# A joint key-and-score product on five stacked arrays of 128 rows in place of six, with the left sides of the mixer on VectorE and the exponentials one step later

## What is computed

```
x = x + xattn(ctx_768, layernorm(x), mask, ...)   # 4 heads of 64; 1601 context tokens of 192 channels per batch
x = x + attn(layernorm(x), ...)                   # token mixer: a recurrence with 4 heads
x = x + ffn(layernorm(x), ...)                    # 16 experts, 4 picked, and a shared one

# xattn, what matters here
xn = layernorm(ctx) * g + b;  ln = layernorm(latents) * g + b
q = ln @ Wq.T;  k, v = [xn @ Wkv.T ; ln @ Wlkv.T] split in halves
attn = rmsnorm(q) * SCALE @ rmsnorm(k).T, masked, softmax over 1601 + 64 keys
out = (attn @ v) @ Wo.T + bo
```

## Time and profile before

| | |
|---|---|
| time, median of 3 runs | 528.2 us (527.94 to 531.03) |
| the profiled execution | 528.14 us, of which the span is 526.4 us |
| mean granted TensorE clock | 0.958 |
| attention loop (first to last `kr`) | 50.8 to 328.1 us |
| token mixer, then experts | about 348 to 439 us, then to the end |
| busy: PE, PEld, DVE, ACT, POOL | 456.7, 358.0, 372.4, 217.5, 269.9 us |
| key-and-score matmuls | 624, of the 828 in the largest PE group |

### The profile page before, as it was taken

The page is one execution under the profiler, slowest core; times in us unless marked ns, Lnnn a source line. Parts: engine busy times, 40 slices in busy tenths (PEclk is TensorE's granted clock), DMA queues, the critical chain, the costliest instruction groups (busy, mean ns, idle before and its releaser), DMA issues.

```text
span 526.4 us, 6598 instructions
## 1 busy us (share of the span) xinstructions
PE 456.7 (87%) x2146; PEld 358.0 (68%) x2146; DVE 372.4 (71%) x850; ACT 217.5 (41%) x471; POOL 269.9 (51%) x261
## 2 busy tenths in 40 slices
PE   3787787998989989989989989788899787789996
PEld 0464555876877877868778768685366665678885
DVE  5746576787887888878876775533568756887776
ACT  0236443554554545654445534231053025335551
POOL 5454868659568576595685543001372232435550
PEclk9999988799999999999999979896999899989999
DMA  7705970051231501514000000920000000000001
GB/s 237 184 1 135 249 183 2 1 140 49 59 82 49 138 9 44 140 50 96 0 2 0 2 0 7 396 108 0 1 0 1 0 0 1 0 2 2 0 2 40
DMA packets 23590, 31.74 MB, mean 60 GB/s; under 512 B 2674, under 2 KB 19268, under 8 KB 23556
## 3 DMA queue, kind: packets, MB, share of 16 engines
q1 hardware_dynamic: 23556, 31.32, 21.3%
HBM read 30.69 MB, written 0.52 MB: 59 GB/s over the span
## 4 chain that ended last, share of the span: by engine, by line
DVE 30%; PE 29%; POOL 25%; issue 11%; ACT 3%; DMA 1%; SPq 0%; DVEq 0%; POOLq 0%; ACTq 0%
PE bank L565 28%; POOL kr L469 16%; DVE kss L1368 5%; DVE arena L1380 5%; DVE arena L1416 5%; POOL crs L440 3%; POOL split_b L463 2%; DVE kguard L1371 2%; DVE arena L1576 1%; DVE arena L1562 1%; DMA mask_in<-in_p_mask 1%; POOL cve L439 1%; POOL cguard L441 1%; DVE arena L1418 1%; DVE cst L1313 1%
## 5 line engine op out<-in xcount | busy, mean ns | idle before, releaser
L565 PE MATMUL bank<-keyq,split_b 96*128 96x512 f32 (+2 forms) x828 | 198.2, 390 | 14.6 <-DVE split_b L1633 9.7
L565 PEld LDWEIGHTS bank<-keyq,split_b 96*128 96x128 f32 (+2 forms) x828 | 147.3, 196 | 47.8 <-DVE split_b L1633 11.6
L469 POOL TENSOR_TENSOR kr<-kguard,neg_half 128x8 f32<-128x8 f32 (+1 forms) x56 | 87.1, 1555 | 95.4 <-DVE kguard L1371 94.9
L565 PE MATMUL bank<-arena 128*128 128x193 f32 (+4 forms) x528 | 104.7, 343 | 11.7 <-ACT arena L1116 6.9
L565 PEld LDWEIGHTS bank<-arena 128*128 128x128 f32 (+2 forms) x528 | 89.0, 198 | 24.2 <-ACT arena L1116 11.3
L1380 DVE TENSOR_TENSOR arena<-bank,kr 128x512 f32<-128x512 f32 (+1 forms) x56 | 36.6, 653 | 58.0 <-POOL kr L469 58.0
L463 POOL TENSOR_TENSOR split_b<-arena,split_b 98x512 fp32r<-98x512 f32 (+1 forms) x56 | 65.4, 1169 | 7.5 <-ACT split_b L1092 7.5
L1116 ACT ACTIVATE arena<-arena 128x512 f32<-128x512 f32 x48 | 30.2, 631 | 75.5 <-DVE arena L1416 75.5
L1109 ACT ACTIVATE arena<-bank 128x512 f32<-128x512 f32 (+1 forms) x56 | 31.5, 563 | 51.3 <-PE bank L565 51.0
L565 PE MATMUL bank<-split_b,keyq 128*128 128x512 f32 x204 | 49.6, 393 | 0.1
L565 PEld LDWEIGHTS bank<-split_b,keyq 128*128 128x128 f32 x204 | 37.5, 190 | 7.4 <-DVE split_b L1624 0.2
(11 more groups left out here) (216 smaller groups left out, 598.7 us busy)
## 6 DMA issues: line engine op xcount, KB each, us to landing
arena<-in_p_ctxT SPq DMA_DIRECT2D x8, 1200.8 KB, 8.8
arena<-in_ctx SPq DMA_DIRECT2D x16, 576.0 KB, 4.9
arena<-in_p_experts SPq DMA_DIRECT2D x1, 2688.0 KB, 18.2
arena<-in_p_experts SPq DMA_DIRECT2D x1, 2304.0 KB, 12.5
arena<-in_p_experts SPq DMA_DIRECT2D x1, 1536.0 KB, 7.1
X<-in_x SPq DMA_DIRECT2D x1, 512.0 KB, 4.1
arena<-in_t_Wlkv SPq DMA_DIRECT2D x1, 512.0 KB, 8.9
out<-arena SPq DMA_DIRECT2D x4, 128.0 KB, 1.8
```

Source lines behind the costliest of these rows:

```text
L469: pool.tensor_tensor(kr[0:r, n % 2, 0:k], kg_[0:r, n % 2, 0:k], neg_half[0:r, 0:4 * k].rearrange("p (t h) -> p t h", h=H), ALU.pow).then_i ...
L565: return nc.tensor.matmul(out_, l, r, start=start, stop=stop, skip_group_check=shared)
```

## The change

**Channels.** The 192 context channels are divided 128 and 64 (`CH`) in place of 96 and 96. The second array holds 64 channels, two rows of the standard deviation (high part and low part, both by DMA), the mask row, zeros up to row 96, and in rows 96 to 127 half of the low part of its own 64 channels. Two such copies exist, one with the lower and one with the upper 32 channels' low part. The weights have matching rows (`twin`, on ACT, copies 32 rows of the high part of keyq to rows 96 to 127). A tile's product then is five matmuls, (high0, high0), (high0, low0), (twin A, twin A), (twin B, low with twin B), (low0, high0), ten per group in place of twelve, each with 128 rows.

**Splitting.** `split_high` is two ACT instructions (128 x 256, and 96 x 512 which writes both copies). `split_rest` is three POOL instructions: 128 x 256, a wait for its own completion, then twice 32 x 256 from partitions 0 to 31 or 32 to 63 into 96 to 127, and a wait again. `sd_low` is new on POOL (13 x 128, at g = 4), `evac_sd` has two ACT instructions, and `spread_sd` has two DMAs and waits for `sd_low`. The turned context and Wkv each come by two DMAs.

**Order.** `SUM` is NG + 4, so exponentials and context_sum come one step later; `evac_sum` moves from g = 2 to g = 3 and `evac_latent_out` from 3 to 4 on DVE; shift_scores follows key_sums at g = 2 and 3. In the mixer the left sides move to DVE, each ahead of the right side of its level; on POOL `gate_up_low(0)`, `gate_up_low(1)` and `down_low(0)` move behind the scales of the group norm, between and behind the two `rstd`.

The core of the diff:

```diff
-        SUM = NG + 3
+        SUM = NG + 4
...
-                pool.tensor_tensor(xs_low[n % 3][:, :, 0:k], ctxT[b % 2][:, :, 256 * g:256 * g + k], xs_high[n % 3][:, :, 0:k].bitcast(F32), ALU.subtract).then_inc(xs_rest, 1)
+                v, raw = xs[n % 3], ctxT[b % 2][:, :, 256 * g:256 * g + k]
+                then(pool.tensor_tensor(v[:, 1, 0:k], raw[:, 0], v[:, 0, 0:k].bitcast(F32), ALU.subtract))
+                for j in range(2):
+                    last = pool.tensor_tensor(v[96:P, 2 + j, 0:k], raw[32 * j:32 * j + 32, 1], v[32 * j:32 * j + 32, 2 + j, 0:k].bitcast(F32), ALU.subtract)
+                last.then_inc(xs_rest, 1)
+                pool.wait_ge(xs_rest, n + 1)
...
+                if g == 4 and b + 1 < B:
+                    sd_low(b + 1)
...
-                    for s, (x_, w_) in enumerate(((xs_high, 0), (xs_low, 0), (xs_high, 1))):
-                        for c in range(2):
-                            d = DEPTH[c]
-                            last = mm(bank[0:rows(t), key_banks(n) + i, :], x_[n % 3][0:d, c, i * P:i * P + rows(t)],
-                                      keyq[0:d, c, w_, 0:slot + 1:slot, :], s == 0 and c == 0, s == 2 and c == 1)
+                    for s, (x_, w_) in enumerate(((0, 0), (0, 1), (2, 2), (3, 3), (1, 0))):
+                        last = mm(bank[0:rows(t), key_banks(n) + i, :], xs[n % 3][:, x_, i * P:i * P + rows(t)],
+                                  keyq[:, w_, 0:slot + 1:slot, :], s == 0, s == 4)
...
-                A(xs_high[n % 3][:, :, 0:k], ctxT[b % 2][:, :, 256 * g:256 * g + k], ACT.Copy).then_inc(xs_split, 1)
+                A(xs[n % 3][:, 0, 0:k], ctxT[b % 2][:, 0, 256 * g:256 * g + k], ACT.Copy)
+                A(xs[n % 3][0:96, 2:4, 0:k], ctxT[b % 2][0:96, 1:2, 256 * g:256 * g + k].broadcast_to([96, 2, k]), ACT.Copy).then_inc(xs_split, 1)
...
-                sp.wait_ge(sdT_evac, b + 1)
+                sp.wait_ge(sd_rest, b + 1)
...
-                if g != 2 and 0 <= u - SHIFT < groups:
+                if g not in (2, 3) and 0 <= u - SHIFT < groups:
                     shift_scores(u - SHIFT)
...
                 if lv + 2 < LEVELS:
+                    left_side(lv + 2)
                     right_side(lv + 2)
```

158 lines of the change are left out of this document (92 added, 66 removed).

## The result

The changed kernel takes **557.0 us** (median of 4 runs, 556.4 to 558.2), the kernel before 529.15 (median of 4): a ratio of 1.054 (95% interval 1.050 to 1.057), 28 us slower. The forecast was 551, with a range of 532 to 575. The profiled execution spans 555.2 us where it was 526.4. Every ratio in this text leaves out executions more than 1.5% above the fastest of their kernel (one of ten of e_moved_by_act_circle, three of ten of e_moved_late), and every median has all of them.

What follows compares the result with a forecast made beforehand. The prediction took the circle of DVE and POOL, not PE, as the bound. Loop 19.4, deviations 4, start 1.3, drain -1.3 and mixer -0.2 summed to +23.2 us on 528.14, so 551, with a range of 532 to 575.

Steps and rivals of the forecast that it cites:

- The split's parts: POOL's split in the attention loop: 0.73 us for each part, narrow ones too, so three take 2.2 against 1.27.
- Full steps with a shift: Attention-loop steps g = 5, 6 and the next 0: each costs 0.24 us more, with DVE's maximum going first.
- g=1 to 2: Loop step where POOL is the longer arm: 0.8 us more in each of seven batches.
- The first batch: First batch of the attention loop, without shifts: 2.2 us more.
- g=2 to 4: Loop steps with the new DVE order, the short split and sd_low: together +0.3 us a batch.
- The rule against the row: Shift of g = 3 during kr: the trace row lets it run at once (551); the port rule holds it (557).
- The deviations' way: DMA of the standard deviations waits for sd_low, making DVE's squares at g = 5 late: 0.6 us in seven batches, 4.
- Start: Chain to the first keys: ACT's extra split instructions and twin copies cost +1.3 us, at most 2.5.
- Drain: End of the loop: PE's wait for an exponential goes with exponentials a step later, -1.3 us.
- win the ties: Rival: POOL's second split part goes ahead of DVE's maximum in about 20 steps, +13 us, so 564; chance 0.18.
- The clock: Rival: PE's granted clock falls in the loop, one episode in each of six batches, +15 us, so 566; chance 0.10.
- Narrow parts: Rival: POOL's 32-row split parts are cheap, 0.3 us each, time near 536 or 531; chance 0.18.

Runs made afterwards that it cites:

- e_moved_by_act_circle: Changed kernel with POOL's low parts in two instructions, ACT copying the 32-row pieces, and DVE's shift and maximum behind the next step's sums: 528.5 us.
- e_moved_late: e_moved_by_act_circle with ACT's copies at the head of its next step and POOL's g=2 scales ahead of its split: 532.9 us.
- e_before_five: Kernel before with the last of the six matmuls of each tile left out: 527.2 us, ratio 0.999.
- e_before_split3: Kernel before with only POOL's split cut into three instructions of 256 elements a row, with waits: 558.6 us, ratio 1.057.
- the split in one: Changed kernel with POOL's three split instructions put together to one of 128 x 512, output differing: 523.3 us, ratio 0.990.
- e_after_no_sdlow: Changed kernel without the low part of the standard deviations, the high part sent twice as soon as ACT has it: 552.2 us, ratio 1.045.
- e_before_circle: Kernel before with DVE's shift and running maximum both behind the next step's key sums: 511.1 us, ratio 0.970.

## Why the prediction was right, point by point

**The bound.** Right: DVE and POOL's circle, not PE. e_before_five shows it by itself, and the waits in both kernels agree.

**Matmuls at nothing.** Right: -0.6 us with an interval of -2.2 to +1.0, in place of 27.

**The split's parts.** Right in size and in the reason for it. By form, from 54 to 356 us (columns: count, busy us, mean ns, idle before). The means hold the waits behind DVE; one alone stands in the timeline with 0.74:

```profile
L472 POOL TENSOR_TENSOR split_b<-arena,split_b 32x256 fp32r<-32x256 f32 x90 | 83.8, 931 | 6.2
...
L470 POOL TENSOR_TENSOR split_b<-arena,split_b 128x256 fp32r<-128x256 f32 x45 | 35.9, 797 | 7.1 <-ACT split_b L1109 7.1
```

```profile
184.38 0.74 POOL L472 TENSOR_TENSOR split_b<-arena,split_b 32x256 fp32r<-32x256 f32 x1
```

A part of 32 partitions takes 0.74 and one of 128 takes 0.73, so the height and the move between partitions cost nothing. e_before_split3 shows that this edit alone makes a loss as large as the change's.

**The loop.** Forecast +23.4 (19.4 and 4 for the deviations), measured +29.9. This is the term that was too small, in three places. (a) Full steps with a shift: 0.24 held for g=4 to 5 (5.17 against 4.92 without the deviations), but g=5 to 6 and 6 to 0 took 0.35 (0.46 in every second batch at 6 to 0). The sum counted on full key sums (0.67) covering POOL's third part; at g=5 to 6 the sums have 65 rows and take 0.40 (timeline above), the third part ends later than they do, and kr waits for it. (b) g=1 to 2: +1.26 in place of 0.8. The sum had the third part end 2.63 behind kr and cve right behind it. The second part is held by the maximum and takes 1.26, and cve starts 2.93 behind kr, 1.73 later than before in place of 1.39. The sum also gave cve 0.4 back, as if it were no longer held. It still is, by the shift, which is itself held by the third part, so cve gives back only 0.12; but cguard, held before, takes 0.26 in place of 0.59, which the sum did not have. So what comes back, 0.45, is right in size by luck, and the parts are what cost more. In the changed kernel:

```profile
175.72 2.06 POOL L472 TENSOR_TENSOR split_b<-arena,split_b 32x256 fp32r<-32x256 f32 x2
177.86 0.57 POOL L445 TENSOR_SCALAR cve<-cmv 128x7 f32<-128x7 f32 x1
...
180.10 0.26 POOL L447 TENSOR_SCALAR cguard<-cve 128x7 f32<-128x7 f32 x1
...
177.10 1.22 DVE L1435 TENSOR_TENSOR arena<-arena,side 128x512 f32<-128x512 f32 x1
```

and before, behind the cve of the earlier trace rows:

```profile
199.12 0.59 POOL L441 TENSOR_SCALAR cguard<-cve 128x7 f32<-128x7 f32 x1
```

(c) The first batch: 37.2 against 31.8, +5.4, where I had 2.2 and 0.6 for the deviations. Without shifts DVE's arm is short, and POOL's three parts are the longer one; 1.3 of the 5.4 goes with the deviations (the batch takes 35.9 without them). Places (a) and (b) make the 4.8 us by which batches two to seven exceed 6 x 3.3, (c) the other 2.6; the last batch, -0.1 in place of +1.0, gives 1.1 back. That last number is luck. In the kernel before, g=3 to 4 of the last batch took 7.15 us with the slow stretch of the earlier trace rows in it, and 4.79 after. Without these 2.4 us, for which the sum had no term, the loop's forecast would have been further off.

**g=2 to 4.** Forecast +0.3, measured +0.09. The price of the parts is +0.49 (e_before_split3), and the new order on DVE, with the shift in the time of kr, gives 0.41 back.

**The rule against the row.** The forecast went by the row (kr doesn't hold the shift) and not by the rule's 557. The row was right about that: g=2 to 3 fell from 5.19 to 4.59 with the move. That the time came out at 557 is no proof of the rule; it is (a) to (c). But the rule's other half, a DVE instruction that holds kr, I had not thought of.

**The deviations' way.** Forecast +4, measured 4.8 by taking it away. The size was right, the path wrong: I had DVE waiting for squares, but it is POOL's first part that waits for ACT's split (shown above). It also isn't a price of its own, as the split in one hides all but 0.27 us in each of the first two batches.

**Start, drain, mixer.** Start: forecast +1.3, measured -0.6 (the first kr stood at 50.0 to 51.1 in the six kernels that start as the one before does, so this is hardly more than their scatter); no cost of the twins' copies shows. Drain: forecast -1.3, measured -0.6 from the last kr to the last sum (23.4 to 22.8). Rest: forecast -0.2, measured +0.2.

**The rivals.** POOL did not win the ties: 32 of the 40 maxima of 128 x 512 ran free in 0.69 us, the others took 0.85; in the step shown the lead was 0.01 us. (The prediction named an unheld maximum as a sign of being wrong. That contradicts its own sum, which has the maximum go first, and by the sum it was right.) The clock did fall, once in every batch from the third on, and cost nothing there. Two stretches of the changed kernel (last columns: granted clock, DMA share, GB/s):

```profile
140.00:150.00 10.00, 8.89 (x32) 7.46 (x33) 7.01 (x16) 2.58 (x8) 8.57 (x12) 0.66 0.24 65
150.00:160.00 10.00, 8.39 (x49) 7.16 (x48) 8.19 (x19) 6.73 (x18) 8.13 (x7) 1.00 0.01 2
```

The steady batches are 39.5 to 39.9 us with it, and DVE waits for squares 3.0 us in the whole loop: slack in PE pays for it. But the cover was thin. In these batches the clock was low for 6.8 us at a time; in e_before_split3 and e_after_no_sdlow, stretches of 10.2 us that reached into g=3 to 4 cost 0.65 to 1.3 each, six times in all. So this rival, with a chance of 0.10, had a mechanism that is real and a price that did not fall due in the changed kernel. Narrow parts were not cheap, and PE was not the bound.

## What to carry to other kernels

Price an engine's relief by who waits for it, not by its busy share: with PE at 87% a sixth of its key matmuls was worth nothing, until two DVE instructions had been moved behind the key sums; then the same cut was worth 11 us. Count the instructions that a rearrangement costs the engines in the circle: on POOL a piece of 32 partitions took 0.74 us and one of 128 took 0.73. And look first for work in the circle that nobody in it waits for, such as the maximum and the shift here: moving these two calls (e_before_circle) gave 17 us and needed no new layout.
